# Perceiver block on one core: the scan's first loads issued during the projections, and routing by two picks and doubling sums

## What is computed

```
x = x + cross_attention(ln(x), ctx, ctx)        # 16 heads, 1601 keys per batch
x = x + mamba(ln(x))                            # scan over the 64 latents (below)
x = x + moe(ln(x))                              # 8 experts, the best 2 of each token

# mamba: xz = x@Win+bin; xs,z = split(xz); xs = silu(xs); xp = xs@Wx+bx -> dp, B, C
#        delta = softplus(dp@Wdt+bdt); for t in 64:
#            h = exp(delta_t*A)*h + (delta_t*x_t)*B_t ;  y_t = sum_n h*C_t     (512 features, 16 states)
#        out = ((y + xs*Dp) * silu(z)) @ Wout + bout
# moe:   logits = x@router_w.T + router_b; p = softmax(logits); w, idx = top_k(p, 2); w /= sum(w)
#        out = sum over the two experts of w * (gelu(x@w1[e].T + b1[e]) @ w2[e].T + b2[e])
```

## Time and profile before

| | |
|---|---|
| median of 3 runs | 2318.96 us |
| profiled execution: its own time | 2319.08 us |
| profiled execution: span shown in the profile | 2317.4 us |
| scan, from its first instruction to the output's Block | 1618.9 to 1906.7 us |
| routing, first instruction to the first of the experts | 1952.3 to 1991.5 us |

### The profile page before, as it was taken

How to read it: one execution, slowest core, us unless ns; L and a number is a source line. 1 busy time by engine, 2 the same in 40 slices (tenths; PEclk the granted TensorE clock), 3 DMA queues, 4 the chain that set the end, 5 groups by cost and what they waited for, 6 DMA issues and landing times. The chain is left out here.

```text
span 2317.4 us, 65069 instructions
## 1 busy us (share of the span) xinstructions
PE 2114.5 (91%) x28676; PEld 1743.9 (75%) x28676; DVE 1432.1 (62%) x2624; ACT 1241.2 (54%) x1680; POOL 763.6 (33%) x566
## 2 busy tenths in 40 slices
PE   6999999999999999999999999696799996599993
PEld 4888889999999999999889988543233336599993
DVE  4555555555555555655555553546788865688885
ACT  2445555555555555555555545166899961355551
POOL 2223222222222232222222220000899961255551
PEclk9999999999999999999999999898899997699997
DMA  3111111111111111111111110214875522466663
GB/s 99 45 40 42 40 48 42 40 48 43 43 53 40 41 49 40 41 49 40 43 46 40 46 30 5 65 55 177 210 175 145 142 64 94 152 214 215 225 228 122
DMA packets 131138, 195.41 MB, mean 84 GB/s; under 512 B 18116, under 2 KB 109252, under 8 KB 130696
## 3 DMA queue, kind: packets, MB, share of 16 engines
q1 hardware_dynamic: 121832, 174.98, 25.1%
q0 software_dynamic: 4416, 12.06, 1.6%
q10 hardware_dynamic: 4608, 4.20, 0.5%
HBM read 159.61 MB, written 31.59 MB: 83 GB/s over the span
## 5 line engine op out<-in xcount | busy, mean ns | idle before, releaser
L543 DVE TENSOR_REDUCE max_part<-work 128x1 f32<-128x384 f32 (+1 forms) x1024 | 534.7, 569 | 179.5 <-PE work L671 156.1
L606 ACT ACTIVATE probs<-scores 128x1024 f32<-128x1024 f32 (+1 forms) x416 | 423.7, 1026 | 334.9 <-PE scores L696 323.4
L497 POOL TENSOR_TENSOR ctx_lo<-ctx_whole,ctx_hi 128x768 fp32r<-128x768 f32 (+1 forms) x128 | 231.4, 1808 | 1024.9 <-DVE ctx_hi L526 1024.9
L538 DVE SCALAR_TENSOR_TENSOR keys_lo<-work,bk,keys_hi 128x384 fp32r<-128x384 f32 (+1 forms) x256 | 162.5, 635 | 330.9 <-ACT keys_hi L585 330.9
L1269 POOL TENSOR_TENSOR decay<-steps_in,xn 128x1024 f32<-128x1024 f32 x126 | 243.4, 1965 | 191.1 <-DMA steps_in<-scratch_results 177.4
L690 PE MATMUL scores<-q_hi,keys_hi 64*128 64x256 f32 (+1 forms) x1664 | 254.2, 284 | 1.6 <-issue 1.1
L690 PE MATMUL scores<-q_lo,keys_hi 64*128 64x256 f32 (+1 forms) x1664 | 249.9, 278 | 1.1 <-issue 1.1
L690 PE MATMUL scores<-q_hi,keys_lo 64*128 64x256 f32 (+1 forms) x1664 | 249.8, 279 | 0.4 <-issue 0.4
L661 PE MATMUL work<-wv_hi,ctx_hi 128*128 128x256 f32 (+1 forms) x832 | 243.6, 293 | 0.2
L661 PE MATMUL work<-wv_hi,ctx_lo 128*128 128x256 f32 (+1 forms) x832 | 234.1, 281 | 0.0
L661 PE MATMUL work<-wv_lo,ctx_hi 128*128 128x256 f32 (+1 forms) x832 | 233.9, 281 | 0.0
(11 more groups left out here) (234 smaller groups left out, 4610.9 us busy)
## 6 DMA issues: line engine op xcount, KB each, us to landing
xs<-in_w_T SPq DMA_DIRECT2D x46, 1024.0 KB, 7.1
ctx_whole<-in_ctx_T SPq DMA_DIRECT2D x96, 384.0 KB, 3.2
steps_in<-scratch_results SPq DMA_DIRECT2D x256, 128.0 KB, 2.7
ctx_whole<-in_ctx_T SPq DMA_DIRECT2D x32, 449.0 KB, 3.4
scratch_results<-steps SPq DMA_DIRECT2D x16, 512.0 KB, 2.6
scratch_mixed<-mixed ACTq DMA_DIRECT2D x32, 128.0 KB, 3.2
scratch_z<-z SPq DMA_DIRECT2D x16, 256.0 KB, 3.6
zg<-scratch_z SPq DMA_DIRECT2D x16, 256.0 KB, 3.2
```

Of the source, the lines that this page charges most:

```text
L497: nc.gpsimd.tensor_tensor(ctx_lo[c][:, :, 0:n], s.ctx_whole[c % 2][:, :, 0:n], ctx_hi[c][:, :, 0:n].bitcast(F32), ALU.subtract).then_inc(l ...
L538: nc.vector.scalar_tensor_tensor(keys_lo[par][:, m, start:start + n], bank[:, 0:n], s.bk[:, m:m + 1], keys_hi[par][:, m, start:start + n]. ...
L543: nc.vector.reduce_max(max_part[par][:, place(pair), c:c + 1], bank[:, 0:CHUNKS[c][1]], AX) \
L606: nc.scalar.activation(probs[n % PROBS][0:rows, :], scores[slot][0:rows, :], ACT.Exp, scale=1.0 / HD ** 0.5).then_inc(exp_done, 1)
```

## The change

1. `b_of`, `c_of` and the first two `steps_in` buffers are allocated before the projections. In the projections SP loads steps 0 and 1 after it has stored chunk 1 (waiting only for chunk 0's stores), stores `bc` before chunk 2's stores, and loads `c_of` and `b_of` after chunk 2's. GpSimd clears `b_of` there. The ring of `log` and `lost` shrinks from 6 to 4.
2. The scan loads from step 2 on. VectorE's order at its start is `b_diag` 0, `a_rest`, the rest of argument 1, `b_diag` 1, `c_diag` 0, `skip`; TensorE waits for `skip` only where it is used.
3. The router's bias is loaded in the output's Block. GpSimd's constants are ordered by first use, and VectorE's first instruction waits for one of them; `zeros` comes last.
4. `chosen` comes from two picks (maximum, equality, rank among equals, on 128x128) in place of the comparison of all pairs. The weights follow from one `gap` per token.
5. `r_total` comes before `r_prefix`; the counts are summed by four doubling additions.
6. Slots are read with the picks themselves; the tile is found by scaling and rounding; `in_tile`, `at_tile` and `in_row` are made in five parts (8, 8, 8, 4, 4), and TensorE takes each part as it is ready.

```diff
 ssm_projections, SyncE
-            for c in range(NCH):
-                ... steps and z of chunk c; bc stored behind those of chunk 2 ...
+            store_steps(0)
+            store_z(0)
+            store_steps(1)
+            store_z(1)
+            sp.wait_ge(first_steps_stored, 16 * CT)
+            for t in range(FIRST):
+                load_step(sp, d, s, t, s.first_in)
+            sp.wait_ge(bc_copied, 2 * NCH)
+            for i in range(2):
+                sp.dma_start(d.bc[i, :, :], xp[32 * (i + 1):32 * (i + 1) + STATE, :]).then_inc(bc_stored, 16)
+            store_steps(2)
+            store_z(2)
+            sp.wait_ge(b_cleared, 1)
+            sp.wait_ge(bc_stored, 32)
+            load_bc(sp, d, s)
+            store_steps(3)
+            store_z(3)
+LOADS, FIRST = 6, 2
 ssm_scan
+                if t >= FIRST:
+                    load_step(sp, d, s, t, steps_in)
...
-            nc.vector.memset(b_of[:, :, :, :], 0.0).then_inc(b_cleared, 1)
-            for k in range(KI):
-                nc.vector.tensor_scalar(skip[:, k, :], s.ident[:, :], s.dp[:, k:k + 1], None, ALU.mult) \
-                    .then_inc(skip_made, 1)
...
+            b_diagonals(0)
             nc.vector.tensor_copy(a_rest, a_rep[:, 2:4, POOL_FEATURES:INNER]).then_inc(a_parted, 1)
             dve.wait_ge(a_parted, 1)
-            b_diagonals(0)
+            rest_of_argument(1)
             b_diagonals(1)
             c_diagonals(0)
-            rest_of_argument(1)
+            for k in range(KI):
+                nc.vector.tensor_scalar(skip[:, k, :], s.ident[:, :], s.dp[:, k:k + 1], None, ALU.mult) \
+                    .then_inc(skip_made, 1)
 route, TensorE
-            nc.tensor.matmul(prefix_bank[:, :], earlier[:, :], flat, start=True, stop=True)
             nc.tensor.matmul(total_bank[:, :], ones[:, :], flat, start=True, stop=True).then_inc(counted, 1)
+            nc.tensor.matmul(prefix_bank[:, :], earlier[:, :], flat, start=True, stop=True).then_inc(counted, 1)
+            for n, (first, last) in enumerate(PARTS):
+                pe.wait_ge(in_row_ready, n + 1)
+                for a in range(first, last):
+                    product = nc.tensor.matmul(slots_bank[:, :, :], in_row[:, a, :], at_tile[:, a, :, :], ...)
 route, VectorE
+            def choose(i, among):
+                then(nc.vector.tensor_reduce(best[i][:, :], among, AX, ALU.max))
+                then(nc.vector.tensor_tensor(score[:, :, :], among, over(best[i][:, :], te), ALU.is_equal))
+                then(nc.vector.tensor_tensor(score[:, :, :], score[:, :, :], across(from_last[:, :], te), ALU.mult))
+                then(nc.vector.tensor_reduce(rank[:, :], score[:, :, :], AX, ALU.max))
+                then(nc.vector.tensor_tensor(pick[i][:, :, :], score[:, :, :], over(rank[:, :], te), ALU.is_equal))
+            dve.wait_ge(s.router_loaded, 32)
+            dve.wait_ge(made, MADE_FIRST)
...
+            choose(0, L)
+            then(nc.vector.scalar_tensor_tensor(others[:, :, :], pick[0][:, :, :], LOWEST, L, ALU.mult, ALU.add))
+            choose(1, others[:, :, :])
+            nc.vector.tensor_tensor(chosen[:, :, :], pick[0][:, :, :], pick[1][:, :, :], ALU.add).then_inc(chosen_ready, 1)
+            nc.vector.tensor_tensor(gap[:, :], best[1][:, :], best[0][:, :], ALU.subtract).then_inc(gap_known, 1)
...
-            for t in range(TT):
-                then(nc.vector.tensor_tensor(counts[:, t + 1, :], counts[:, t, :], total_bank[:, t * E:(t + 1) * E],
-                                             ALU.add))
+            then(nc.vector.tensor_copy(a[:, PAD:, :], total_bank[:, :].rearrange("p (t e) -> p t e", e=E)))
+            for into, of, back in ((b, a, 1), (a, b, 2), (b, a, 4), (a, b, 8)):
+                then(nc.vector.tensor_tensor(into[:, PAD:, :], of[:, PAD:, :], of[:, PAD - back:PAD + TT - back, :], ALU.add))
...
+            for i in range(2):
+                then(nc.vector.tensor_tensor(hit[i][:, :, :], pick[i][:, :, :], place[:, :, :], ALU.mult))
+            for i in range(2):
+                then(nc.vector.tensor_reduce(slot[:, :, i], hit[i][:, :, :], AX, ALU.add))
+            then(nc.vector.tensor_scalar(tile[:, :], slots, 1.0 / P, -half, ALU.mult, ALU.add))
+            then(nc.vector.tensor_scalar(tile[:, :], tile[:, :], WHOLE, -WHOLE, ALU.add, ALU.add))
+            nc.vector.scalar_tensor_tensor(slots, tile[:, :], -float(P), slots, ALU.mult, ALU.add).then_inc(step, 1)
+            for first, last in PARTS:
+                ... in_tile (is_equal), at_tile 0 and 1, in_row of these columns; in_row_ready + 1 ...
+            dve.wait_ge(exped, 1)
+            ... total = gap + 1, weight 0 = 1 / total, weight 1 = gap * weight 0 ...
             dve.wait_ge(slots_found, 1)
```

More of the change, by code:

```diff
@@ L1527, in route @@
         block_index = sb("block_index", [P, BLOCKS])
+        from_last = sb("from_last", [P, E])
         logits = sb("logits", [P, TT, E])
[L1529 to L1532, removed]
+        others = sb("others", [P, TT, E])
+        score = sb("score", [P, TT, E])
+        rank = sb("rank", [P, TT])
+        best = [sb(f"best{i}", [P, TT]) for i in range(2)]
+        pick = [sb(f"pick{i}", [P, TT, E]) for i in range(2)]
+        hit = [sb(f"hit{i}", [P, TT, E]) for i in range(2)]
+        gap = sb("gap", [P, TT])
+        total = sb("total", [P, TT])
         chosen = sb("chosen", [P, TT, E])
-        total = sb("total", [P, TT])
-        counts = sb("counts", [P, TT + 1, E])
+        counts = [sb(f"counts{i}", [P, PAD + TT, E]) for i in range(2)]
         filled = sb("filled", [P, E, MAX_NB])
@@ L1590, in _, with count @@
         def _(pool):
-            nc.gpsimd.memset(zeros[:, :], 0.0).then_inc(zeros_made, 1)
+            def count(out, pattern, base, multiplier):
+                nc.gpsimd.iota(out[:, :], pattern=pattern, base=base, channel_multiplier=multiplier,
+                               allow_small_or_imprecise_dtypes=True).then_inc(made, 1)
+            count(from_last, [[-1, E]], E, 0)
+            for c in counts:
+                nc.gpsimd.memset(c[:, 0:PAD, :], 0.0).then_inc(made, 1)
             nc.gpsimd.memset(earlier[:, :], 1.0).then_inc(made, 1)
@@ L1627, in _ @@
-            for a in range(2 * TT):
-                if a % 8 == 0:
-                    pe.wait_ge(in_row_ready, a // 8 + 1)
-                last = nc.tensor.matmul(slots_bank[:, :, :], in_row[:, a, :], at_tile[:, a, :, :],
-                                        start=(a == 0), stop=(a == 2 * TT - 1))
-            last.then_inc(slots_found, 1)
+            nc.tensor.matmul(prefix_bank[:, :], earlier[:, :], flat, start=True, stop=True).then_inc(counted, 1)
+            for n, (first, last) in enumerate(PARTS):
+                pe.wait_ge(in_row_ready, n + 1)
+                for a in range(first, last):
+                    product = nc.tensor.matmul(slots_bank[:, :, :], in_row[:, a, :], at_tile[:, a, :, :],
+                                               start=(a == 0), stop=(a == 2 * TT - 1))
@@ new lines, in _ @@
+            done[0] += 1
+            for first, last in PARTS:
+                part = slice(first, last)
+                at, row = [P, last - first, SLOT_TILES], [P, last - first, P]
+                then(nc.vector.tensor_tensor(in_tile[:, part, :], over(tile[:, part], at), across(tile_index[:, :], at),
+                                             ALU.is_equal))
+                nc.vector.tensor_tensor(at_tile[:, part, 0, :], in_tile[:, part, :], over(tile_number[:, part], at), ALU.mult)
+                nc.vector.tensor_scalar(at_tile[:, part, 1, :], in_tile[:, part, :], partition[:, 0:1], None, ALU.mult)
+                nc.vector.tensor_tensor(in_row[:, part, :], over(slots[:, part], row), across(row_index[:, :], row),
+                                        ALU.is_equal).then_inc(in_row_ready, 1)
@@ L1737, in _ @@
+            dve.wait_ge(exped, 1)
+            then(nc.vector.tensor_scalar(total[:, :], gap[:, :], 1.0, None, ALU.add))
+            then(nc.vector.reciprocal(s.weight[:, 0, :], total[:, :]))
+            nc.vector.tensor_tensor(s.weight[:, 1, :], gap[:, :], s.weight[:, 0, :], ALU.mult)
             dve.wait_ge(slots_found, 1)
```

188 lines of the change are left out of this document (78 added, 110 removed).

## The result

The changed kernel took 2300.01 us (median of 4 runs, 2295.68 to 2304.04) where the kernel before took 2318.93 (4 runs): ratio 0.9915, 95% interval 0.9902 to 0.9928, so faster by 0.85%. That is 16.7 to 22.7 us less; 22.4 had been forecast, and a median of 2296.6. With the runs made later for the experiments it is 2298.2 (14 runs) against 2318.9 (34 runs), 20.8 us less; one further execution of the kernel before took 5527 us, far outside all others, and is left out everywhere.

The account below looks back on a forecast made before the run. Bounds taken: idle engines at the scan's start, step 6's load as second gate, and the routing's VectorE chain. Gains of 8.3 + 14.1 = 22.4 us against the median of 2318.96 gave 2296.6 us; range 2293 to 2302.

Parts of the forecast that it names:

- Loads in the projections: SP's queue in the projections: the added loads fit in holes of 8.6 and 14.8 us and are charged nothing.
- The second gate: Scan, step 6's load on the DMA queue: arrives 8.3 us earlier, which limits the scan's gain to 8.3 us.
- the lower bound I had named: Scan's gain if the queue follows SP's issue of 16 DMAs before the stores: never less than 7.4 us.
- The upper bound: Scan's gain: never more than the 9.8 us by which GpSimd can begin earlier.
- Computing, moved by 9.8 us: Scan, GpSimd: computing shifted 9.8 us earlier would want step 6's load at 1639.9, before its arrival at 1641.4.
- The first `keep` at 4.5 us: Scan's start, VectorE: the first keep comes at 1623.4 in place of 1633.20, with the scan starting at 1618.9.
- So my sum has nothing for it: Scan's start: no charge for skip beside GpSimd's products, as a cast overlapping GpSimd's work lost only 0.08 us.
- My rival: Scan's start: each skip waits out a GpSimd product, first keep near 1629.9, total gain 17.4 us, 2301.6; chance 0.07.
- Routing 14.1 us: Routing, VectorE's chain and TensorE's products: readout begins at 1975.5 in place of 1989.62, 14.1 us earlier, bounds 12 to 15.
- the parts and the last products: Routing: five parts take 10.24 us on VectorE, then TensorE's last four products 0.88 + 0.15 us.
- Transfers under the routing: Routing's end: the weights should be in by 1975 and the routing ends near 1977.5, covered by 2.5 us.
- TensorE's clock: Scan, slower rival: the clock stays at half, 0.67 us more per step, 2339 if at all steps; chance 0.02.

Follow-up runs that it names:

- experiment 7: Changed kernel with skip made in the projections and the transfers of z, wout, bout and x_tok spread over later scan steps: median 2294.78 us, ratio 0.9892.
- again: The changed kernel run again with no edit: median 2298.29 us (5 runs), ratio 0.9915.
- experiment 5: Changed kernel with skip made in the scan by a two-tensor product, one operand (dp, widened) in PSUM: scan 280.2 us.
- experiment 4: Changed kernel with the four skip diagonals made in the projections, where GpSimd idles (also written skip_early): median 2297.00 us (4 runs).
- route_only: Kernel before with only the router's earlier bias load and the new routing: median 2306.20 us (5 runs), ratio 0.9946.
- experiments 8 and 9: Changed kernel with the router's bias loaded at the routing's start (bias_late): routing 27.6 us; with in_tile and at_tile in one piece (whole_tiles): routing 26.6 us.
- after: First profiled execution of the changed kernel, no edit: 2295.68 us, scan 280.0, routing 25.7.
- again2: The changed kernel run once more with no edit: median 2296.99 us (5 runs).
- scan_only: Changed kernel with output and routing taken from the kernel before: median 2311.48 us (11 runs), ratio 0.9971.
- stores_later: Changed kernel with wout, bout, the store of x_tok and two z loads moved from behind step 5's loads to behind step 9's: scan 277.8 us.
- before: First profiled execution of the kernel before, no edit: 2319.08 us, scan 287.7, routing 39.1.
- before_again: A second profile of the kernel before, no edit: scan 287.8 us, routing 39.1.

## Why the prediction was right, point by point

- **Loads in the projections cost nothing:** right. Chunk 3's stores stand as far before the scan as they did, and GpSimd's first scan product comes with the barrier.
- **The second gate:** right, and it is what made the number. I had 8.3 us from the queue starting earlier, against 9.8 from the engines; the profiles' means give 8.2, their medians 7.9. In the first profile step 6 comes 7.5 us earlier: SP issued everything behind step 5 at 7.5 us less (1624.29 - 1616.96 = 7.3 in place of 14.8), which fits the lower bound I had named, the issue. With a scatter of 2 us the profiles do not tell 8.3 from this bound, so the close hit of 8.3 is partly luck. The upper bound was too low. "Computing, moved by 9.8 us" took over the 1.79 us that GpSimd had waited for step 6 in the kernel before; without this wait it could start step 6 up to 11.6 us earlier, and in experiment 7, with no gate, step 6 came 11.3 us earlier (19.4 in place of 30.7). Step 6 was forecast at 22.5 us after the scan's start and came at 23.2, with the wait of about 3 us that I had foreseen (3.14).
- **The first `keep` at 4.5 us:** wrong in the changed kernel, 6.5 to 6.6 in three profiles with this start and 7.9 in again; it was 4.4 in three others, where a product held only one `skip`. The failed step is "So my sum has nothing for it", my reading of the earlier trace rows. The cast there lasted 0.08 us more than its mean beside an overlap of 0.23, and I took this as proof of an overlap without a lock. The overlap was too short to tell. A held `skip` ended 0.08 us behind its product, though alone it takes 0.27, so about 0.19 us of it go by before the wait begins to lengthen it; an estimate from this leaves a cast with an overlap of 0.23 us only some 0.04 us to lose under a full lock, where 0.08 were seen. And the cast was not the one like pair of that trace, as I had written. In the output stage of the kernel before, one `ln_rstd` of 12 started beside GpSimd's products:

```profile
L140 DVE TENSOR_SCALAR ln_rstd<-ln_mean_var x12: 169/169/1419, 6.6 to 1941.7; 128x4 f32<-128x4 f32 x12
```

```profile
1914.25 3.46 POOL L1464 TENSOR_TENSOR x_tok<-x_tok,win 128x256 f32<-128x256 f32 x5
...
1916.31 1.42 DVE L140 TENSOR_SCALAR ln_rstd<-ln_mean_var 128x4 f32<-128x4 f32 x1
```

It took 1.42 us where the others take 0.17, and ended 0.02 us behind the last of the products (1917.71). This row, read before the change, would have shown the lock.

The Trainium skill (SBUF — State Buffer, "Who interferes with whom") was right on this against my reading: the scalar form waits, the form with one operand in SBUF and one in PSUM does not (experiment 5). My rival was wrong in its prices. It had 6.5 us of delay, all four held in turn; the measured one is 2.1 to 3.5, as two or three were held, and none where one was. And it let the delay of the first `keep` pass whole into the scan, where GpSimd's lead took up most of it. It cost nothing in the end, because the gate came later still (experiment 4).

- **Routing 14.1 us:** mechanism right, size 0.6 too large: 13.5, from 39.1 in all three profiles with the old routing to 25.7 in those with the new one (25.3 in route_only; the edits of experiments 8 and 9 apart). VectorE began 0.56 us after the stage's start and not 0.22: GpSimd's first count ran 0.3 us late. The rest is in the parts, where the scalar `at_tile` took 0.41 against 0.37. The single terms held: the bias 2.0 of a forecast 2.3, `filled` 7.1 us earlier (7.45), the parts and the last products 11.7 (11.4).
- **Transfers under the routing:** right; nothing waited for the weights, with 1.3 us to spare where I had 2.5.
- **TensorE's clock:** it did not stay low. In the first profile it stood at 2.4 GHz from 11 us after the scan's start on (from about 28 before); in skip_early only from about 25. Step 6 started 0.07 us behind the landing of its load in both, at 23.2 and 23.4, so the clock did not set it.
- **The median:** the sum by stages is 8.2 + 13.5 = 21.7, the runs give 20.8, the first four 18.9. My sum was made beside a profile whose attention was the longest: 1419.7 us, where 12 of the 13 others lie between 1415.4 and 1417.4. Of the 1.6 us between the forecast 22.4 and the 20.8 of the runs, 0.6 are the routing's and 0.1 the scan's. The remaining 0.9, between 21.7 and 20.8, is within the runs' spread, and I have not settled it.

## What to carry to other kernels

When a start is moved earlier, look for the next late arrival on the same queue: here the engines could start 9.8 us earlier, and the scan became some 8 us shorter, about as far as the transfers ahead of step 6's load had moved. One table of when GpSimd got step 6 against the stage's length told more than all whole times. And when an instruction is moved beside another engine's work, ask in which form it runs and where its operands lie: the same result, made by a product with one operand in PSUM, never waited for GpSimd. Before a short overlap is taken as proof against a lock, look through the trace for the longest member of every group of that form.

## What the runs showed of the hardware that I had not expected

- A scalar-form product of 0.27 us on VectorE, SBUF to SBUF, lasted up to 2.45 us beside GpSimd's products, and how many of four were held (one to three) differed between executions of like code. Which are held follows from the order of starts (experiment 5). A product that held one hardly got longer, 2.35 to 2.41 us in after, again, again2 and bias_late; where the fourth `skip` had begun 0.02 to 0.04 us before a product (scan_only, whole_tiles, stores_later) the product took 2.45 to 2.48.
- Two stages come in two lengths, with either kernel's code in them: the projections take 115.4 to 115.6 or 116.7 to 116.9 us (before 115.6, route_only with the same code 116.8 and before_again 115.6), the attention's output 51.1 to 51.6 or 51.9 to 52.2. What picks the one or the other stays open.
